# A normalised 7x7 convolution: GpSimd issues the loads of units 4 to 15 on its software queue, SyncE the stores alone

## The reference

```python
def _gn(v, G=32, eps=1e-05):
    ...
    return ((g - m) / jnp.sqrt(s + eps)).reshape(v.shape)
kern = construct_kernel(weight, P)            # (32, 32, 7, 7)
out = conv(_gn(x), kern, padding=3) + bias[None, :, None, None]
return x + out
```

## Time and profile before

| what | value |
|---|---|
| median of three runs | 327.74 us |
| the three runs | 327.01, 330.44, 327.74 us |
| span of the profiled execution | 324.2 us |
| median of the runs less that span | 3.5 us |
| TensorE busy | 289.6 us (89% of the span) |
| VectorE busy | 273.1 us (84%) |
| ScalarE busy | 218.6 us (67%) |
| GpSimd busy | 155.0 us (48%) |

### The profile page before, as it was taken

How to read it: one execution, slowest core, us unless ns; L and a number is a source line. 1 busy time by engine, 2 the same in 40 slices (tenths; PEclk the granted TensorE clock), 3 DMA queues, 4 the chain that set the end, 5 groups by cost and what they waited for, 6 DMA issues and landing times.

```text
span 324.2 us, 9588 instructions
## 1 busy us (share of the span) xinstructions
PE 289.6 (89%) x3380; PEld 201.7 (62%) x3380; DVE 273.1 (84%) x454; ACT 218.6 (67%) x327; POOL 155.0 (48%) x259
## 2 busy tenths in 40 slices
PE   5920589999999989999999989999999999999990
PEld 2700466666666657776677766677877666766760
DVE  4489598999898888989899989989998989897331
ACT  2369796967868676967696788778796868461300
POOL 6232545645363727374564527372929274644000
PEclk9975599999999999999999999999999999999997
DMA  8953354989898896979797989999898939489605
GB/s 141 151 110 85 88 140 96 255 196 242 186 217 215 195 236 146 265 167 255 156 259 173 237 189 193 254 189 255 168 260 176 262 78 243 107 223 235 135 12 99
DMA packets 128253, 59.07 MB, mean 182 GB/s; under 512 B 122068, under 2 KB 122068, under 8 KB 128228
## 3 DMA queue, kind: packets, MB, share of 16 engines
q1 hardware_dynamic: 115204, 24.90, 40.9%
q0 software_dynamic: 9312, 33.04, 36.8%
q10 hardware_dynamic: 3712, 0.80, 1.4%
HBM read 12.88 MB, written 12.85 MB: 79 GB/s over the span
## 4 chain that ended last, share of the span: by engine, by line
PE 57%; DVE 9%; SPq 9%; issue 8%; DMA 7%; POOL 3%; ACT 3%; DVEq 0%; ACTq 0%; POOLq 0%
PE ps_s L802 17%; PE ps_x L802 16%; PE ps_y L802 12%; PE ps_eo L802 8%; SPq L196 6%; DMA xraw<-x 4%; DVE e L451 3%; SPq L186 3%; DVE d L451 2%; DMA xb<-xs 2%; DVE xs L472 2%; POOL xn L702 2%; PE ps_eo L770 1%; POOL xb L690 1%; DMA wnat<-L_conv_weight 1%
## 5 line engine op out<-in xcount | busy, mean ns | idle before, releaser
L690 POOL DMA_DIRECT2D xb<-xs x192 | 93.5, 494 | 62.0 <-DVE xs L472 59.3
L802 PE MATMUL ps_s<-xb,w 128*64 128x392 f16 (+1 forms) x576 | 103.4, 329 | 0.9 <-DMA xb<-xs 0.8
L802 PE MATMUL ps_s<-xs,w 128*64 128x392 f16 (+1 forms) x576 | 103.9, 329 | 0.2 <-ACT m L349 0.2
L702 POOL TENSOR_SCALAR xn<-xraw,scale,offset 32x784 f32<-32x784 f32 x32 | 55.0, 1724 | 79.3 <-DVE offset L448 79.3
L802 PEld LDWEIGHTS ps_s<-xs,w 128*64 128x64 f16 x576 | 62.4, 110 | 22.0 <-issue 1.5
L802 PEld LDWEIGHTS ps_s<-xb,w 128*64 128x64 f16 x576 | 62.3, 110 | 9.2 <-DMA xb<-xs 2.2
L802 PE MATMUL ps_x<-xs,w 128*64 128x392 f16 x384 | 66.5, 329 | 0.1
L802 PE MATMUL ps_x<-xb,w 128*64 128x392 f16 x384 | 66.6, 329 | 0.0
L343 ACT ACTIVATE xs<-e 128x900 f16<-128x900 f32 x48 | 59.1, 1230 | 10.3 <-DVE e L451 6.4
L802 PE MATMUL ps_eo<-xb,w 128*64 128x392 f16 (+1 forms) x384 | 65.5, 326 | 0.0
L802 PE MATMUL ps_eo<-xs,w 128*64 128x392 f16 (+1 forms) x384 | 65.5, 326 | 0.0
(11 more groups left out here) (90 smaller groups left out, 403.7 us busy)
## 6 DMA issues: line engine op xcount, KB each, us to landing
xb<-xs POOLq DMA_DIRECT2D x96, 168.8 KB, 4.1
xb<-xs POOLq DMA_DIRECT2D x96, 166.9 KB, 4.4
xraw<-x SPq DMA_DIRECT2D x124, 98.0 KB, 2.9
out<-result SPq DMA_DIRECT2D x124, 98.0 KB, 5.0
xraw<-x ACTq DMA_DIRECT2D x4, 98.0 KB, 3.9
out<-result ACTq DMA_DIRECT2D x4, 98.0 KB, 3.7
wnat<-L_conv_weight POOLq DMA_DIRECT2D x1, 36.0 KB, 3.8
pts<-L_conv_P POOLq DMA_DIRECT2D x2, 1.1 KB, 3.1
```

The lines of the kernel that those rows point to most:

```text
L690: pool.dma_start(dst[32 * g:32 * g + 32, 0:run - line * past], src[32 * f:32 * f + 32, line * past:run]).then_inc(shifted[par][b], DMA)
L702: pool.tensor_scalar(xn[96:128, u % 2, :, SLOTS * m:SLOTS * m + ROWS, 1:1 + SIDE // 2], image(u % RING, m)[96:128, :].rearrange("p (n w k) ...
L802: last = pe.matmul(into[p:p + HALF, :, 0:PER * wide], w[:, n // 2, s, q, t, :], moving.rearrange("p n q m -> p n (q m)"), start=fresh and ...
```

## The change

GpSimd issues the loads of units 4 to 15. They stand in its iterations 1 to 12, behind the four DMAs of `shift(u, ., 0)` and ahead of `normalise(u + 1)`; a wait for the second seed of unit u-1 precedes them. SyncE keeps the loads at the start (units 0 to 3) and issues the stores of its loop with no loads between them. The refills count on semaphores of their own (`x_refilled`).

```diff
@@ -184,7 +185,7 @@
         def fetch(queue, u, r, m, g):
             queue.dma_start(image(r, m)[32 * g:32 * g + 32, :].rearrange("c (n w) -> c n w", w=SIDE),
-                            dram_rows(x, u, m, g)).then_inc(x_loaded[r], DMA)
+                            dram_rows(x, u, m, g)).then_inc((x_loaded if u < RING else x_refilled)[r], DMA)
...
@@ -278,11 +279,7 @@
             with sp.Fori(0, UNITS // RING - 1) as it:
                 for h in range(RING):
-                    u = it * RING + h
-                    sp.wait_ge(seeded, 2 * u + 2)
-                    sp.wait_ge(last_group_normalised, NORMS * u + NORMS)
-                    load(u + RING, h)
-                    store(u, h % 2)
+                    store(it * RING + h, h % 2)
...
             def sums(u, r, nth):
-                act.wait_ge(x_loaded[r], LOAD * (nth + 1))
+                if isinstance(nth, int) and nth == 0:
+                    act.wait_ge(x_loaded[r], LOAD)
+                else:
+                    act.wait_ge(x_refilled[r], LOAD * nth)
...
             normalise(0)
+            def load(u):
+
+                pool.wait_ge(seeded, 2 * (u - RING) + 2)
+                for m in range(PER):
+                    for g in range(GROUPS):
+                        fetch(pool, u, u % RING, m, g)
+
             for u in range(UNITS):
                 shift(u, u % 2, 0)
+                if 0 < u and u + RING - 1 < UNITS:
+                    load(u + RING - 1)
                 if u == 0:
                     shift(u, u % 2, 1)
                 if u + 1 < UNITS:
```

More of the change, by code:

```diff
@@ L124, in build @@
         x_loaded = [sem(f"x_loaded_{r}") for r in range(RING)]
+        x_refilled = [sem(f"x_refilled_{r}") for r in range(RING)]
         stored = [sem("stored_even"), sem("stored_odd")]
```

## The result

| kernel | median | span of the profiled execution | step, second seed to second seed, units 0 to 12 |
|---|---|---|---|
| before | 328.31 us (4 runs) | 324.2 us | 17.43 us |
| changed | 344.57 us (4 runs) | 342.2 us | 18.62 us |

The changed kernel takes 1.0475 times as long as the kernel before, 95% interval 1.0405 to 1.0546. The ratio leaves out runs in a slower state (one of the changed kernel's four), so it is not the ratio of the two medians. The kernel before has four runs now, one more than when the prediction was made; hence 328.31 us. The time was inside the range and on the forecast side, but the loss is half of the one forecast: 16.3 us (18.0 of span) in place of 33.7.

A forecast was written before the change was run, and what follows sets the result against it. A chain from second seed through GpSimd's loads and normalisation and ScalarE was to bound the kernel: 12 x 20.24 = 242.9 us replaces 209.2, +33.7 on span 324.2 gives 357.9, plus 3.5 makes 361 us; range 334 to 392.

The forecast's parts named there:

- the third bound: Second seed, GpSimd's normalisation, ScalarE, next second seed: 16.32 us before the change, 1.1 us to spare; loads go into it.
- Forecast step 20.24: Second seed to second seed: eight loads at 0.75, then 0.1, 2.85, 0.08 and 11.21 us, in place of 17.43.
- The price of a load, t = 0.75: GpSimd's time to issue one 448-row load: 0.75 us, ends 0.49 and 1.04, eight per step ahead of the normalisation.
- The normalisation, 2.85: GpSimd's two instructions behind the loads, taken as one slow and one fast: 2.85 us, ends 2.09 and 3.60.
- ScalarE's part, 11.21: ScalarE from the first stream after GpSimd's normalisation to its next second seed: 11.21 us, as in the earlier trace.
- stream 4 of unit 12: At the tail, TensorE starts it about 3.5 us before unit 12's second seed ends, as in the kernel before.
- TensorE waited for copies: TensorE waits 3.4 us a step for shifted copy 1, in twelve steps, without lengthening the step.
- priced the clock at nothing: TensorE's clock does not fall in its new gaps, so it adds 0 us; a fall would show the prediction wrong.
- The first (t = 1.04): Rival: each load costs GpSimd 1.04 us or more, step 22.56, total 389 us; chance 0.24.
- The second (rows cost nothing, t = 0.49): Rival: each load costs GpSimd only 0.49 us whatever its rows, step 18.15, total 336 us; chance 0.20.
- The third, that the ring closes in the old time: Rival: load at 0.49 and normalisation at 2.09 us, step 17.39, not slower, 327 us; chance 0.07.
- SyncE as a second bound: SyncE's queue spends some 16.7 us of each step issuing loads and stores, as long as TensorE; relief worth at most 8.4 us.

The follow-up runs named there:

- experiment 1: Kernel before, plus only GpSimd's wait for the second seed of unit u-1 ahead of the normalisation, all loads on SyncE: 330.72 us against 331.32 before.
- experiment 2: Kernel before with that seed wait and eight GpSimd memsets of 600 elements behind it, loads on SyncE: 333.73 us, 1.0134 times before.
- experiment 9: Changed kernel with each GpSimd load cut into two of 224 rows, 16 issues per unit, same bytes: 393.79 us, one run.
- experiment 4: Changed kernel with four of a unit's eight loads on GpSimd and four on SyncE ahead of the stores: 323.72 us, 0.9808 times before.
- experiment 3: Changed kernel with GpSimd's eight loads behind the normalisation instead of ahead of it: 368.17 us, 1.1163 times before.
- experiment 5: Changed kernel with two of a unit's eight loads on GpSimd and six on SyncE: 321.04 us, 0.9748 times before.
- experiment 8: Changed kernel with two of a unit's eight loads on GpSimd, six on SyncE, and two of its eight stores also on GpSimd: 320.25 us, 0.9763 times before.

## Why the prediction was right or wrong

**Right: the third bound.** The ring over GpSimd and ScalarE, its place, and the order of events came out as put. Experiments 1, 2 and 9 show it: the wait alone shows no cost, time on GpSimd without any load costs, and 4.4 us more of issues in the ring lengthen the step by 4.2. The traffic of the loads on the software queue is not needed for the loss.

**Wrong in size: three terms of the ring.** Forecast step 20.24, measured 18.62; over twelve steps 223.4 us in place of 242.9, 19.4 less.

- *The price of a load, t = 0.75.* It was 0.633, worth 8 x 0.12 = 0.94 us a step. The step that failed is the slope of 0.62 ns a row between a shifted copy (0.489, SBUF to SBUF) and a 96-row load from HBM. The two HBM rows alone, 0.51 and 0.53, give 0.3 ns a row and 0.64 us. Three prices for reads of HBM now stand: 0.51 at 32 rows, 0.592 at 224, 0.633 at 448. I mixed two kinds of transfer in one slope, and from 32 to 448 rows no single slope fits: 0.43 ns a row up to 224, 0.18 beyond.
- *The normalisation, 2.85.* It was 2.16, worth 0.69 us a step. I took one instruction slow and one fast; both ran fast. While it ran from 150.74 to 152.90 in the changed kernel, VectorE did this:

```profile
149.54 1.02 DVE L476 SCALAR_TENSOR_TENSOR part<-ps_s,scales,eo 128x784 f32<-128x784 f32 x1
151.91 1.16 DVE L476 SCALAR_TENSOR_TENSOR result<-ps_y,scales,part 128x392 f32<-128x392 f32 x2 [1.34 <-PE ps_y L811]
```

  Each of these reads an operand from PSUM. In the kernel before, subtractions of two SBUF operands (L472) stood beside the 3.60 us of the earlier trace rows. The Trainium skill (SBUF — State Buffer, "SBUF: two separate sides") names that pair: a VectorE operation with two SBUF inputs and a GpSimd operation that reads SBUF exclude each other. The traces agree. The pair took 3.60 us beside two subtractions (0.69 and 1.17 us), 3.08 in experiment 4 beside the second of them alone, and 2.16 beside none; and that second subtraction, 1.17 us before, took 1.71 in the same place of experiment 4. No run changed VectorE's work alone.
- *ScalarE's part, 11.21.* It was 10.96; the row of 11.21 held a wait of 0.16 for VectorE (L451) that is gone in the step shown above. The hand-over from seed to load took 0.29, not 0.1.

**Missed: the ends.** The start was 0.7 us later, and from the second seed of unit 12 to the end it took 66.9 us in place of 63.9. I had said stream 4 of unit 12 would start 3.5 us before that seed ends; it started 0.35 before, so TensorE left the ring further behind. (In the twelve steps TensorE waited for copies as forecast, but 14.6 us in 11 places in all, 1.3 each and not 3.4.) The chain at that place:

```profile
265.78 5.46 DMA xb<-xs
271.25 0.04 issue
271.29 3.40 PE ps_s L811 x23
```

and windows of the same trace, the first behind an earlier wait, the others around this one:

```profile
66.60:70.60 4.00, 4.00 (x38) 2.51 (x36) 1.92 (x3) 3.66 (x5) 0.29 (x2) 0.66 0.94 266
...
270.00:271.20 1.20, 0.00 (x0) 0.00 (x0) 1.20 (x2) 1.20 (x5) 1.20 (x3) 0.80 1.04 273
271.20:272.00 0.80, 0.71 (x6) 0.43 (x8) 0.80 (x2) 0.80 (x2) 0.65 (x2) 0.50 0.94 276
```

TensorE had waited 2.3 us for the copy, and the clock was at 0.50 when it went on: 3.40 us for a stream of 1.92, 1.5 of the 3 us. The copy itself took 5.46 us to land, over a us more than the medians of 4.0 and 4.3. The prediction priced the clock at nothing, and named a fall of it as a sign of being wrong. It fell twice: behind the wait that ended at 66.16 (2.17 us) and behind this one (2.31). At the other waits for a copy that lasted 0.9 us or more, six of 0.97 to 1.80 us, it stayed at 1.00. The step behind the first fall took 19.45 us in place of 18.5; in the other steps the price of nothing held, and at the end it did not. The length of the wait does not settle it: in experiment 3 waits of 2.46 us were followed by 0.50 and waits of 2.38, 2.72 and 3.47 us by 1.00. Why is open. Together: 33.7 - 19.4 + 0.7 + 3.0 = 18.0 us, the span's difference. On top of the span the prediction put 3.5 us; in the changed kernel's run it was 2.4.

**The rivals.** The first (t = 1.04) is refuted by 0.633. The second (rows cost nothing, t = 0.49) is refuted too, though the Trainium skill's sentence (DMA: Bandwidth & Descriptors, "Anatomy of one DMA") was the better guide to size: 416 rows more added 0.12 us. The third, that the ring closes in the old time, had its short normalisation (2.16) but not its load price; six loads are where it happened, 0.997 times before. The idea behind the change, SyncE as a second bound, is borne out: with SyncE relieved and the ring kept short, 2 to 2.5% were won (experiments 4, 5 and 8).

## What to carry to other kernels

Before moving work to an engine with idle time, find which part of that idle time lies behind the event for which the moved work waits. Here GpSimd idled 79 us before its normalisations, but only 1.4 to 1.8 us per step of it came after the seed, room for two loads and not eight. And where an engine's queue stands in more than one ring, follow each branch to the engine's next turn: moving the loads behind the normalisation left the first ring and closed a longer one.

## What the runs showed of the hardware

- A DMA issued by GpSimd costs a nearly fixed time on that engine: 0.489 us for 32 rows of SBUF, 0.592 for 224 rows and 0.633 for 448 rows of 224 bytes from HBM. The same load on SyncE's queue took 0.56 us in the kernel before (median), and 0.74 with the address arithmetic around it (5.93 us for eight).
- Loads on the software queue made fewer packets: 88316 in all after the change, 128253 before, for the same 59 MB.
- The two normalisation instructions of GpSimd took 3.60, 3.08 or 2.16 us, with two, one or none of VectorE's subtractions of two SBUF operands beside them (kernel before, experiment 4, changed kernel).
- TensorE's clock stood at 0.50 for some 3 us behind two waits of 2.17 and 2.31 us in the changed kernel, and a stream of 1.92 us took 3.40. Behind waits of up to 1.80 us it stayed at 1.00 there; in experiment 3 it did so behind one of 3.47 us too.
